# Second retention's end: table loads, the order of two lanes and the fillers of a one-core two-layer kernel

## The reference

```python
h = layernorm(x, ln1_w, ln1_b)
h = silu(h_prev * conv_w[:, 0] + h * conv_w[:, 1])
q, k, v, g = silu(h @ Wq), h @ Wk, h @ Wv, h @ Wg
scores = softmax(einsum('bhld,hdr->bhlr', v, router_w))
idx = argmax(scores)
o = einsum('bhlm,bhmd->bhld', qk, v)
o = (o - mu) * rsqrt(var + EPS)
o = silu(g) * o
attn_out = o @ Wout + residual
h2 = layernorm(attn_out, ln2_w, ln2_b)
out = silu(h2 @ w1) * (h2 @ w3) @ w2 + attn_out
...
probs = softmax(xf @ router_w.T)
top_w, top_i = top_k(probs, 2)
h = gelu(einsum('nc,ech->enh', xf, w1), approximate=False)
y = einsum('enh,ehc->enc', h, w2)
out = einsum('ne,enc->nc', comb, y)
```

## Time and profile before

| what | value |
|---|---|
| median of 3 runs | 281.15 us (279.26 to 281.96) |
| the profiled execution | 281.34 us |
| its span on the core | 279.6 us |
| PE busy | 235.5 us, 84% of the span |
| DVE busy | 191.2 us, 68% |
| ACT busy | 128.1 us, 46% |
| POOL busy | 43.2 us, 15% |

### The profile page before, as it was taken

One profiled execution on the slowest core, in us unless ns is written; L12 is line 12 of the kernel. 1 busy time (PEld: TensorE's weight loads), 2 busy tenths in 40 slices (PEclk: granted clock), 3 DMA queues, 4 the chain that ended last, 5 costly groups with the idle time before them and its releaser, 6 DMA issues.

```text
span 279.6 us, 4964 instructions
## 1 busy us (share of the span) xinstructions
PE 235.5 (84%) x1885; PEld 171.5 (61%) x1885; DVE 191.2 (68%) x550; ACT 128.1 (46%) x274; POOL 43.2 (15%) x65
## 2 busy tenths in 40 slices
PE   8858676957869679699995998759878999999995
PEld 8445453635434565244592564437666999999995
DVE  6998899587578667979866768785779655424111
ACT  1377785644161106233305955762424564363331
POOL 6000000000100038367320001210350010100000
PEclk9999998695597999999999999986995999999999
DMA  6970000003980300000000000000000000000000
GB/s 179 356 295 1 2 4 0 2 2 83 438 382 1 147 6 0 2 0 0 0 4 1 2 2 1 1 2 0 4 0 0 0 4 0 2 0 19 2 0 19
DMA packets 5564, 13.74 MB, mean 49 GB/s; under 512 B 2081, under 2 KB 3745, under 8 KB 4898
## 3 DMA queue, kind: packets, MB, share of 16 engines
q1 hardware_dynamic: 4096, 10.73, 10.3%
q10 hardware_dynamic: 1442, 2.66, 2.9%
HBM read 13.13 MB, written 0.26 MB: 48 GB/s over the span
## 4 chain that ended last, share of the span: by engine, by line
PE 60%; DVE 23%; ACT 9%; issue 4%; POOL 1%; DMA 1%; DVEq 0%; ACTq 0%
PE BK L2329 11%; PE BK L2344 10%; PE BK L2109 7%; PE BK L2212 3%; PE BK L2185 3%; ACT WTF L750 3%; PE BK L2196 2%; DVE WTF L1370 2%; PE BK L1932 2%; PE BK L2136 2%; DVE WTF L1215 2%; PE BK L1829 2%; PE BK L2058 2%; ACT WTF L821 1%; PE BK L2041 1%
## 5 line engine op out<-in xcount | busy, mean ns | idle before, releaser
L2329 PE MATMUL BK<-XT,WTF 128*128 128x256 f32 x128 | 32.8, 404 | 0.0
L2344 PEld LDWEIGHTS BK<-WTF 128*128 128x128 f32 x256 | 30.9, 192 | 0.8
L906 ACT ACTIVATE WTF<-BK 128x512 f32<-128x512 f32 x32 | 18.9, 598 | 26.4 <-PE BK L2329 26.4
L2344 PE MATMUL BK<-WTF 128*128 128x128 f32 x256 | 31.0, 275 | 0.0
L2109 PE MATMUL BK<-XT,WTF 128*128 128x512 f32 x64 | 28.7, 594 | 0.0
L2329 PEld LDWEIGHTS BK<-XT,WTF 128*128 128x128 f32 x128 | 25.0, 205 | 3.2
L1724 DVE SCALAR_TENSOR_TENSOR X<-BK,CW,X 128x128 f32<-128x128 f32 x32 | 9.7, 346 | 24.7 <-PE BK L2344 24.7
L750 ACT ACTIVATE WTF<-BK 128x512 f32<-128x512 f32 x40 | 22.6, 601 | 7.1 <-PE BK L1915 7.0
L597 POOL TENSOR_TENSOR RSTD<-VE,MHALF 128x2 f32<-128x2 f32 x8 | 5.6, 710 | 103.9 <-DVE VE L1043 103.1
L821 ACT ACTIVATE WTF<-BK,MN 128x128 f32<-128x128 f32 x64 | 18.0, 394 | 6.7 <-DVE MN L1469 6.7
L2109 PEld LDWEIGHTS BK<-XT,WTF 128*128 128x128 f32 x64 | 12.0, 190 | 14.1 <-issue 12.8
(11 more groups left out here) (309 smaller groups left out, 457.7 us busy)
## 6 DMA issues: line engine op xcount, KB each, us to landing
WTF<-w_f_dram SPq DMA_DIRECT2D x2, 2048.0 KB, 14.5
WTF<-w_c_dram SPq DMA_DIRECT2D x1, 2048.0 KB, 7.7
...
```

The lines of the kernel that those rows point to most:

```text
L906: act.activation(GT[:, e % 2, 2 * p:2 * p + 2, lane_cols(h)], lane_bank(h, 2 + p).rearrange("p (a n) -> p a n", a=2), ACT.Gelu).then_inc(e ...
L2329: ins = pe.matmul(lane_bank(h, 2 + p)[:, 256 * i:256 * i + 256], w_f1[:, o:o + P], XT[:, lane_cols(h)], start=True, stop=True)
L2344: ins = pe.matmul(lane_bank(h, e % 2)[:, i * P:(i + 1) * P], GT[:, e % 2, j, b * P:(b + 1) * P], w, start=(j == 0), stop=(j == 3))
```

## The change

It touches only the order of calls, except for two activations that are added, one argument of `rotate`, one of `values`, and the count of filler matmuls:

- ScalarE: a one-column Sqrt activation behind `exponentials(15)` and a one-column Gelu activation behind `deviation(0)`, each of which makes the compiler put the table's load there. `gate_ff(0)` is split around `gate_xT(1)`. `last_xT(0)` and `gelu(0, 0)` stand ahead of `between(1)`, and `route(0)` behind `gelu(0, 1)`. Steps of lane 1 stand one expert later.
- TensorE: `values(3)` is cut in two, with `turn_context(0)` and `project_context(0)` in between. The 8 fillers ahead of the norm's transposes go, the 13 behind `ff_down(0)` become 10. Lane 1's steps stand one expert later.
- VectorE: `attended(0)` ahead of `divide(3)`, and `lane_norm(LN_E2, 0)` ahead of `looked_up(1)`; `lane_norm(LN_F, 0)` directly behind `finished(0)`; `chances(0)` ahead of `shares(1)`, `centred(1)` ahead of `best_two(0)`, `weigh(0, 1)` ahead of `contexts(1)`.
- GpSimd: `lane_power(LN_F, 0)` inside `rotate(1)`, behind its first operation.

```diff
--- before.py
+++ after.py
@@ -643,11 +643,13 @@
                     halves = lambda a: a.rearrange("p b (n f i) -> p b n f i", f=2, i=2)
                     flat = lambda a: a.rearrange("p b a n -> p b (a n)")
 
-                    def rotate(h):
+                    def rotate(h, meanwhile=None):
                         pair = lane_pair(h)
                         qk, qr, q2 = flat(QK[:, pair]), flat(QR[:, pair]), flat(Q2[:, pair])
                         pool.wait_ge(l_q, h + 1)
                         settle(pool.tensor_tensor(qr, qk, cs[:, 0, pair], ALU.mult))
+                        if meanwhile:
+                            lane_power(*meanwhile)
                         for b in range(2):
                             for f in range(2):
                                 settle(pool.tensor_tensor(halves(q2)[:, b, :, f, :], halves(qk)[:, b, :, 1 - f, :],
@@ -665,8 +667,7 @@
                     lane_power(LN_E2, 0)
                     lane_power(LN_E, 1)
                     bypass(0)
-                    rotate(1)
-                    lane_power(LN_F, 0)
+                    rotate(1, (LN_F, 0))
                     lane_power(LN_E2, 1)
                     bypass(1)
                     lane_power(LN_F, 1)
@@ -930,35 +931,39 @@
                     exponentials(14)
                     turned(13)
                     exponentials(15)
+                    act.activation(VM[:, :], col("eps"), ACT.Sqrt)
                     turned(14)
                     turned(15)
                     square(0)
                     deviation(0)
+                    act.activation(VM[:, :], col("eps"), ACT.Gelu)
                     context(0)
                     second_xT(0)
+                    gate_ff(0, (0,))
                     gate_xT(1)
-                    gate_ff(0)
+                    gate_ff(0, (1, 2))
                     take_qkvg(1)
+                    last_xT(0)
+                    gelu(0, 0)
                     between(1)
-                    last_xT(0)
+                    gelu(0, 1)
                     route(0)
-                    gelu(0, 0)
-                    gelu(0, 1)
                     square(1)
                     gelu(0, 2)
                     deviation(1)
                     gelu(0, 3)
+                    gelu(0, 4)
                     context(1)
-                    gelu(0, 4)
+                    gelu(0, 5)
                     second_xT(1)
-                    gelu(0, 5)
+                    gelu(0, 6)
                     gate_ff(1)
-                    gelu(0, 6)
+                    gelu(0, 7)
                     last_xT(1)
-                    gelu(0, 7)
-                    route(1)
                     for e in range(NE):
                         gelu(1, e)
+                        if e == 1:
+                            route(1)
 
 
         @block.vector
@@ -1772,43 +1777,44 @@
                     bypass(0)
                     variances(0)
                     contexts(0)
+                    attended(0)
                     divide(3)
-                    attended(0)
+                    lane_norm(LN_E2, 0, CT)
                     looked_up(1)
                     first_stats(1)
-                    lane_norm(LN_E2, 0, CT)
                     lane_norm(LN_E, 1, X)
                     convolve(1)
+                    gated_ff(0, (0,))
                     gated_xT(1)
-                    gated_ff(0)
+                    gated_ff(0, (1, 2))
                     gated_q(1)
                     finished(0)
+                    lane_norm(LN_F, 0, X)
                     choices(1)
+                    chances(0)
                     shares(1)
-                    lane_norm(LN_F, 0, X)
                     gate_out(1)
                     weights(1)
-                    chances(0)
                     outputs(1)
+                    centred(1)
                     best_two(0)
-                    centred(1)
                     bypass(1)
                     variances(1)
                     weigh(0, 0)
+                    weigh(0, 1)
                     contexts(1)
-                    weigh(0, 1)
                     weigh(0, 2)
+                    weigh(0, 3)
                     attended(1)
                     lane_norm(LN_E2, 1, CT)
-                    weigh(0, 3)
+                    weigh(0, 4)
                     gated_ff(1)
-                    weigh(0, 4)
+                    weigh(0, 5)
                     finished(1)
                     lane_norm(LN_F, 1, X)
-                    weigh(0, 5)
-                    chances(1)
                     weigh(0, 6)
                     weigh(0, 7)
+                    chances(1)
                     best_two(1)
                     for e in range(NE):
                         weigh(1, e)
@@ -2196,7 +2202,7 @@
                             ins = pe.transpose(turn_bank(n)[:, h * P:(h + 1) * P], SS[:, b % 2, 4 * g + h, :], ident[:, :])
                         ins.then_inc(d_pT_ps, 1)
 
-                    def values(b):
+                    def values(b, cs=(0, 1)):
                         pe.wait_ge(d_pT, (2, 4, 8, 12)[b])
                         if b < 2:
                             pe.wait_ge(d_pT2, 2 * b + 2)
@@ -2204,14 +2210,15 @@
                             pe.wait_ge(d_blk, B + 2)
                         if b == 3:
                             pe.wait_ge(d_om, 3)
-                        for c in range(2):
+                        for c in cs:
                             for j in range(4):
                                 for g in range(4):
                                     o = 32 * g
                                     lhs = ONEH[:, 0, 32 * j:32 * j + 32] if c else VMD[:, 4 * b + g, 32 * j:32 * j + 32]
                                     ins = pe.matmul(value_bank(b)[o:o + 32, c * P:(c + 1) * P], lhs, PT[:, b % 2, 4 * g + j, :],
                                                     start=(j == 0), stop=(j == 3))
-                        ins.then_inc(d_o_ps, 1)
+                        if cs[-1]:
+                            ins.then_inc(d_o_ps, 1)
 
                     def project_keys(h):
                         wo_d = w_d[:, 3 * D:4 * D]
@@ -2391,17 +2398,17 @@
                     turn(13)
                     turn(14)
                     turn(15)
-                    values(3)
+                    values(3, (0,))
                     turn_context(0)
                     project_context(0)
+                    values(3, (1,))
                     project_keys(1)
-                    stay_warm(3, 8)
                     lane_norm_T(LN_E2, 0, 1)
                     lane_norm_T(LN_E, 1, 1)
                     ff_up(0)
                     project_qkvg(1)
                     ff_down(0)
-                    stay_warm(3)
+                    stay_warm(3, 10)
                     lane_norm_T(LN_F, 0, 0)
                     logits(0)
                     pe.wait_ge(loads["w_f1"], 16)
@@ -2412,24 +2419,24 @@
                     up(0, 2)
                     down(0, 1)
                     up(0, 3)
+                    down(0, 2)
+                    up(0, 4)
                     turn_context(1)
-                    down(0, 2)
+                    down(0, 3)
                     project_context(1)
-                    up(0, 4)
-                    down(0, 3)
+                    up(0, 5)
+                    down(0, 4)
                     lane_norm_T(LN_E2, 1, 1)
-                    up(0, 5)
+                    up(0, 6)
                     ff_up(1)
-                    down(0, 4)
+                    down(0, 5)
                     ff_down(1)
-                    up(0, 6)
-                    down(0, 5)
-                    lane_norm_T(LN_F, 1, 0)
                     up(0, 7)
                     down(0, 6)
+                    lane_norm_T(LN_F, 1, 0)
+                    down(0, 7)
                     logits(1)
                     up(1, 0)
-                    down(0, 7)
                     for e in range(NE):
                         if e + 1 < NE:
                             up(1, e + 1)
```

## The result

The changed kernel takes 286.85 us (median of 6 runs, 284.56 to 289.26), the kernel before 281.19 us (6 runs, 279.26 to 282.7): a ratio of 1.020, 95% interval 1.014 to 1.026 (medians are of all runs of a kernel, ratios of those within 1.5% of its fastest). It is 2% slower; I had forecast 282.9, 0.6% slower, and a range up to 285.6. The profiled execution after took 288.09 us, its span 286.3.

The account below looks back on a forecast made before the run. TensorE's unbroken expert work was taken as the bound, entered at `down(0, 2)`; 0.9 us for VectorE's chain plus 0.85 for the clock gave about +1.8 on 281.15, 282.9 us. Range 279.3 to 285.6, the forecast's own 281.6 to 284.3.

Parts of the forecast that it names:

- The place of the end: Edits before about 225 us count only by when TensorE enters its unbroken expert work, taken as `down(0, 2)`.
- Part 1, tables: Sqrt's load ahead of `turned(14)` makes `values(3)` 1.6 us later and `contexts(0)` ready 0.8 us later.
- rival (c): Every table load drains, 1.38 us more per load on the path: 285.7 us, chance 0.03.
- Part 2, values halved: Halving `values(3)` makes good the 0.8 us lost at `project_context(0)`, but delays `looked_up(1)` and `ff_up(0)` by 1.85 us.
- 1.85 us later: `looked_up(1)` at 197.6 instead of 195.74, behind `attended(0)`, `divide(3)` and the last four matmuls of `project_keys(1)`.
- rival (b): Three drops: half of `values(3)` is too little work to restore the clock; +4.5 us, 285.6, chance 0.24.
- Part 3, fillers gone: Without `stay_warm(3, 8)` the clock is 1.2 GHz when `ff_up(0)` starts: 1.0 us lost (bounds 0 and 2.5).
- Part 4, norm in front: Norm at `finished(0)` comes earlier, TensorE's pause falls from 2.2 to 0.9 us; `up(0, 0)` at 212.2 against 212.03.
- Part 5: `shares(1)` waits 1.65 us for `between(1)`, TensorE stands 2.8 us before `up(0, 3)`; `down(0, 2)` 0.9 plus 0.85 us later.
- half of the 1.7 us: 0.85 us taken for a possible clock drop at `up(0, 3)`, which would delay `down(0, 2)` by up to 1.7 us.
- My 0.9 us for VectorE's chain: `weigh(0, 0)` on VectorE ends at 226.2, so `down(0, 2)` starts 0.9 us later than 225.29.
- Part 6: Lane 1's steps one expert later, behind `down(0, 2)`, cost nothing; up to 1 us if the gelus' cover is gone.

Follow-up runs that it names:

- e8: Changed kernel with Sqrt's load and one-column activation behind `turned(14)` instead of ahead of it: 285.75 us, ratio 1.011 to the kernel before.
- e12: Changed kernel run again unaltered, for a second trace: 287.51 us against 281.62 for the kernel before, ratio 1.015.
- e9: Kernel before with only `values(3)` halved and VectorE's order to match: 283.02 us, ratio 1.012 to the kernel before.
- e1: Kernel before with only LN_F's norm and power of lane 0 in front, `chances(0)` ahead of `shares(1)`: 280.12 us, ratio 0.995.
- e2: Changed kernel with `values(3)` whole again and VectorE's old order there: 281.91 us, ratio 1.005 to the kernel before.
- e4: Kernel before without the 8 fillers `stay_warm(3, 8)`, nothing else: 283.06 us against 280.95, ratio 1.000.
- e5: e1 with lane 1's steps behind lane 0's third expert one expert later: 281.75 us (4 runs, no usable interval).
- e6: e5 with `best_two(0)` directly behind `gate_out(1)`, `weigh(0, 0)` ahead of `bypass(1)`, `gelu(0, 2)` ahead of `square(1)`: 279.24 us, ratio 0.995 to the kernel before.
- e10: Changed kernel with the edits of e2 and e3, and `gelu(0, 2)` ahead of `square(1)`: 281.53 us, ratio 0.997 to the kernel before.
- e11: e10 with the 8 fillers back and Sqrt's load and activation behind `turned(14)`: 277.44 us, ratio 0.984 to the kernel before.
- e13: e11 with e6's order on VectorE: 283.74 us, ratio 1.013 to the kernel before.
- e14: e11 with 13 fillers instead of 10 behind `ff_down(0)`: 277.81 us, ratio 0.992 to the kernel before.
- e15: e1 with 10 fillers instead of 13 behind `ff_down(0)`: 281.77 us, ratio 0.997 to the kernel before.
- e3: Changed kernel with `between(1)` ahead of `last_xT(0)` and `gelu(0, 0)` again: 283.09 us, ratio 1.002 to the kernel before.
- e7: Changed kernel with the 8 fillers `stay_warm(3, 8)` put back: 283.97 us, ratio 1.011 to the kernel before.

## Why the prediction was wrong

**The place of the end** was right: `down(0, 2)` comes 4.71 us later, the tail is 4.87 us longer.

**Part 1, tables: right.** `values(3)` 1.52 us later against 1.6, `project_context(0)` unchanged. The Trainium skill, page "ScalarE: Activation LUTs", section "What ACT_TABLE_LOAD costs", adds a drain of about 1380 ns to the load; here the activation starts 0.02 us behind the load (187.99 + 1.28 = 189.27, 189.29), so rival (c) is out. Moving the load behind `turned(14)` (e8) gained 1.4 us at `looked_up(1)` against the first trace of the changed kernel and 0.4 against the second, and at the end 0.15 and 0.03.

**Part 2, values halved: right mechanism, mis-sized.** The step that failed is the assumption behind "1.85 us later": that TensorE is back at 2.4 GHz from 193 us on, as before. It was at 1.2 GHz until 207.9. `looked_up(1)` came 3.79 us later (2.81 in e12), and e9, this part alone, gives 3.10. The path to it was another too: I had it run through `attended(0)` and `divide(3)` on VectorE, and it ran through TensorE, where the sums, the bias and eight matmuls of `project_keys(1)` at 1.2 GHz lasted from 196.23 to 201.32 us. I had named just this as rival (b), "`values(3)`'s half is too little work", and given it 0.24. The rows of all traces, start of `values(3)` to the return of the clock:

| `values(3)` | us until the granted clock is 1.00 again |
|---|---|
| whole | before 4.7, e1 4.8, e2 3.4, e4 3.9, e5 11.8, e6 11.7, e10 3.5, e11 3.2, e13 4.7, e14 4.8, e15 3.8 |
| halved | after 16.0, e12 6.6, e3 6.6, e7 6.7, e8 18.4, e9 11.6 |

Nine of eleven whole ones are back within 5 us, none of the halved ones within 6.5. It is a shift of odds, not a rule: e5 and e6, with whole values and the code of before up to `ff_down(0)`, took nearly 12 us.

**Part 3, fillers gone: right mechanism, mis-sized.** From `ff_up(0)` to `ff_down(0)` it is 5.66 us after and 4.45 before: 1.21 us more, forecast 1.0. But that is the smallest of the seven traces without the fillers, because the clock came back in the middle of `ff_up(0)`; in e12 it is 6.57, 2.12 more, and alone 1.36 more (e4). `ff_up(0)` took 4.29 to 5.33 us in all seven traces without the 8 fillers and 2.75 to 2.86 in all ten with them. The Trainium skill, page "TensorE: Matmul & The Clock Gate", section "What's actually happening", calls the throttled clock the default that activity releases; these seven and ten traces agree.

**Part 4, norm in front: right in place.** The norm starts 0.88 us behind its statistics (213.61 to 214.49; forecast 0.8), and the clock held through the first experts in both traces of the changed kernel. That the shorter pause is why it held, I can't say: with the norm in front it fell in e1, e5, e6, e13, e14 and e15 and held in after, e2, e3, e7, e8, e10, e11 and e12.

**Part 5: right in place, the clock under-priced.** The wait of `shares(1)` was 1.91 us (forecast 1.65), TensorE's pause 2.58 (forecast 2.8), and `up(0, 3)` took 3.66 (forecast 3.3 if the clock drops). I had taken half of the 1.7 us; in all five traces with this pause (after, e2, e7, e8, e12) the clock fell behind it. My 0.9 us for VectorE's chain was not on the path: `down(0, 2)` came with the end of `up(0, 3)`, 1.2 us behind that of `weigh(0, 0)`. **Part 6: right**, nothing lost.

**The sum.** `down(0, 2)` was forecast at 42.1 and came at 45.1. Of the 3.0 us between, 1.94 arise up to `looked_up(1)` (part 2's clock), 0.4 from there to `ff_down(0)`, 0.35 from there to `up(0, 0)`, 0.3 in part 5 (14.84 us forecast from `up(0, 0)` to `down(0, 2)`, 15.16 measured). Nothing behind hid any of it, as forecast. The second trace, e12, splits it otherwise: 0.95 up to `looked_up(1)`, and 1.3 from there to `ff_down(0)`, where the clock, back at 198.1, fell again at 201.6. So the failed step is the state of the clock ahead of `ff_down(0)`, in part 2 first and, by the second trace, as much in part 3: `ff_down(0)`, forecast at 21.3, came at 23.7 and 23.6. The cause is that I took the clock's return at 193 us over from the trace of before, though the change takes away half of the very work that stood ahead of this return. Rival (b) is the one that e12 shows fall by fall, and it had a quarter of the chance. I gave it as +4.5 and 285.6, but its own terms (-0.05 without any fall, 0.6 to 1.0, 2.5, 1.7) add up to 4.75 to 5.15, 285.9 to 286.3. The tails are 4.87 and 4.75 us longer, and so good a sum is in part luck: the first fall cost 1.94 and 0.95 us in the two traces, the second 1.2 and 2.1, the third about 1.2 (the 0.85 I took and 0.3 more). The medians lie 5.7 and 5.9 us apart; the 1 us beyond the tail's 4.9 is less than what the stretch ahead of it scatters by, and no run shows what it is.
